# Where the inputs of a sign-weight MLP are made: before the MLP, or inside the attention ahead of it

## What is computed

```
x = x + cross_attention(layernorm(x), ctx, mask)      # x0
x = x + self_attention(layernorm(x))                  # s0: 16 heads of 32
x = x + sign_mlp(layernorm(x))                        # f0: the MLP of this change
x = x + cross_attention(layernorm(x), ctx)            # x1
x = x + causal_self_attention_rope(layernorm(x))      # s1
x = x + quantised_gated_mlp(layernorm(x))             # f1
```

```
h = concat([x, -x]);  h = relu(s0 * (h @ sign(k0))) * 2      # 1024 -> 2048
h = relu(s1 * (h @ sign(k1))) * 2                            # 2048 -> 2048
y = s2 * (h @ sign(k2))                                      # 2048 -> 512
layernorm(x) = (x - mean) / sqrt(var + 1e-5)
```

## Time and profile before

| what | us |
|---|---|
| median of three runs (lowest to highest) | 1258.74 (1256.92 to 1258.98) |
| span of the profiled execution, first to last instruction | 1256.4 |
| first self-attention, from its turn 0 to the last statistics | 201.5 to 317.3 |
| inputs of the sign MLP | 317.3 to 340.3 |
| its first layer on the first half | 340.3 to 379.6 |

### The profile page before, as it was taken

How to read it: one execution, slowest core, us unless ns; L and a number is a source line. 1 busy time by engine, 2 the same in 40 slices (tenths; PEclk the granted TensorE clock), 3 DMA queues, 4 the chain that set the end, 5 groups by cost and what they waited for, 6 DMA issues and landing times. The chain is left out here.

```text
span 1256.4 us, 18017 instructions
## 1 busy us (share of the span) xinstructions
PE 1117.3 (89%) x6536; PEld 684.3 (54%) x6536; DVE 597.6 (48%) x1030; ACT 364.9 (29%) x982; POOL 176.2 (14%) x173
## 2 busy tenths in 40 slices
PE   8999979998489999999998999968799999994986
PEld 4544437777234444444443655538477877863542
DVE  3133117888682111331111344337857566577766
ACT  1211124544221010121010122234333324245874
POOL 1011001110750000000000101104303131300004
PEclk9999988999589999999999999988899999997999
DMA  9964601000310000000001877833000000007001
GB/s 345 387 230 179 241 12 65 1 0 0 117 50 1 0 0 1 0 1 0 0 0 45 332 268 268 332 108 128 1 1 0 0 0 0 0 0 261 16 1 67
DMA packets 55122, 108.53 MB, mean 86 GB/s; under 512 B 4144, under 2 KB 4528, under 8 KB 55088
## 3 DMA queue, kind: packets, MB, share of 16 engines
q1 hardware_dynamic: 55088, 108.09, 24.0%
HBM read 105.98 MB, written 2.10 MB: 86 GB/s over the span
## 5 line engine op out<-in xcount | busy, mean ns | idle before, releaser
L1339 ACT ACTIVATE f_act<-bank,f_sgn 128x512 f32<-128x512 f32 x64 | 44.0, 687 | 273.6 <-PE bank L1296 258.0
L1296 PE MATMUL bank<-f_a_lo,f_w 128*128 128x512 f16 x512 | 115.7, 379 | 0.0
L1296 PE MATMUL bank<-f_a_hi,f_w 128*128 128x512 f16 x512 | 115.7, 379 | 0.0
L1392 DVE CAST f_b_hi<-f_act 128x512 f32 x32 | 13.7, 427 | 181.3 <-ACT f_act L1339 181.3
L962 ACT ACTIVATE s_e<-bank,s_nmax 128x64 f32<-128x64 f32 x256 | 76.0, 345 | 53.8 <-DVE s_nmax L1047 53.3
L1296 PEld LDWEIGHTS bank<-f_a_lo,f_w 128*128 x512 | 50.1, 98 | 60.4
L1296 PEld LDWEIGHTS bank<-f_a_hi,f_w 128*128 x512 | 50.1, 98 | 60.4
L526 POOL TENSOR_TENSOR x_mv<-x_mv,eps 128x2 f32<-128x2 f32 x8 | 1.5, 192 | 511.3 <-DVE x_mv L419 511.3
L1134 DVE TENSOR_TENSOR s_e<-s_pair,s_tables 128x512 f32<-128x512 f32 x64 | 41.3, 687 | 42.1 <-POOL s_kT L1197 24.8
L513 DVE TENSOR_TENSOR xres<-bank,xres 128x512 f32<-128x512 f32 (+1 forms) x16 | 11.1, 691 | 105.3 <-PE bank L332 91.5
L962 ACT ACTIVATION_READ_ACCUMULATOR s_e<-bank,s_nmax 128x1 f32 x256 | 60.9, 239 | 0.0
(11 more groups left out here) (259 smaller groups left out, 2232.1 us busy)
## 6 DMA issues: line engine op xcount, KB each, us to landing
x_cT<-in_ctx_cols_dram SPq DMA_DIRECT2D x32, 1024.0 KB, 7.6
x_cN<-in_ctx_rows_dram SPq DMA_DIRECT2D x32, 1024.0 KB, 10.0
f_upper_bits<-in_f_w_dram SPq DMA_DIRECT2D x20, 256.0 KB, 2.7
f_raw<-in_f_wd_dram SPq DMA_DIRECT2D x1, 2816.0 KB, 18.0
x_qw<-in_x_qw_dram SPq DMA_DIRECT2D x8, 256.0 KB, 4.2
x_kw<-in_x_kw_dram SPq DMA_DIRECT2D x8, 256.0 KB, 5.1
x_vw<-in_x_vw_dram SPq DMA_DIRECT2D x2, 1024.0 KB, 14.5
s_wk_ahead<-in_s_wk_dram SPq DMA_DIRECT2D x1, 2048.0 KB, 14.3
```

The lines of the kernel that those rows point to most:

```text
L1296: mm = pe.matmul(h_bank[s][:, :], weights(2 * i + s, k), part[:, k, cols], start=(n == 0 and k == 0), stop=(n == 1 and k == k_chunks - 1))
L1339: act.activation(act32[s][:, :], h_bank[s][:, :], ACT.Relu, scale=sgn[:, layer % 2:layer % 2 + 1]).then_inc(h_read, 1)
L1392: dve.tensor_copy(hi[:, 2 * i + s, :], act32[s][:, :]).then_inc(hhi_ok, 1)
```

## The change

Six of the eight tiles of the sign MLP's input are made inside s0. The statistics of the two tiles that a turn has finished are aggregated at the end of that turn on VectorE (new: a separating memset ahead of each statistics instruction, which the second self-attention gets too, one more memset, and two aggregations). At the start of the next turn GpSimd takes the root and normalises the two tiles into a new buffer `fn`; TensorE transposes them between the query and the value projections, into banks 2 and 3; ScalarE copies them to `fT_hi` after the queries; VectorE subtracts into `fT_lo` after `layernorm` and before the score maxima. TensorE waits for that before the scores of the second tile, which use the same banks. The last turn no longer normalises, transposes and splits tiles 0 and 1. Tiles 6 and 7 are normalised by GpSimd at the start of the sign MLP, and transposed, copied and split between layers 0 and 1 of the first half. GpSimd's order in s0 changes too: the root for the next turn's rows now stands ahead of the bias additions of this turn. s1 keeps its order but for the memsets.

```diff
@@ self_attention @@
+        F_BANK = [2, 3]
 @block.tensor
-            with pe.Fori(0, TILES // 2) as i:
+            def transpose_signs(n):
+                for s in range(2):
+                    pe.wait_ge(fn_ok, 2 * n + s + 1)
+                    for k in range(KC):
+                        mm = pe.transpose(bank[F_BANK[s]][:, k * P:(k + 1) * P], fn[s][:, k * P:(k + 1) * P], ident[:, :])
+                    mm.then_inc(fT_done, 1)
+            def turn(i, first, last):
...
                 project_transposed(i, PB, wq_hi, wq_lo, q_done, NB if rope is not None else base)
+                if sign_inputs is not None and not first:
+                    transpose_signs(i - 1)
...
                 if rope is None:
+                    if not first:
+                        pe.wait_ge(flo_ok, 2 * i)
                     scores(i, 1, range(GROUPS))
...
-                    transpose_x(i + 1)
+                    if not last:
+                        transpose_x(i + 1)
 @block.scalar
+                    if not first:
+                        for s in range(2):
+                            act.wait_ge(fT_done, 2 * i + s - 1)
+                            act.copy(fT_hi[:, :, bass.ts(2 * i + s - 2, P)], as_chunks(bank[F_BANK[s]][:, :])).then_inc(fhi_ok, 1)
 @block.vector
-                    layernorm(next_first, i + 1)
+                    if not last:
+                        layernorm(2 * i + 2, i + 1)
+                    if not first:
+                        for s in range(2):
+                            at = bass.ts(2 * i + s - 2, P)
+                            dve.wait_ge(fhi_ok, 2 * i + s - 1)
+                            dve.tensor_tensor(fT_lo[:, :, at], bank[F_BANK[s]][:, :].rearrange("p (k n) -> p k n", k=KC),
+                                              fT_hi[:, :, at], ALU.subtract).then_inc(flo_ok, 1)
...
-                    split_x(i + 1)
+                    if not last:
+                        split_x(i + 1)
...
                 for s in range(2):
                     dve.wait_ge(x_ok, 2 * i + s + 2)
-                    dve.bn_stats(core.stats[:, 2 * i + s, :], xres[:, 2 * i + s, :]).then_inc(next_stats, 1)
+                    dve.memset(core.spare[:, 4 + s:5 + s], 0.0)
+                    kept = core.stats[:, 2 * i + s, :] if sign_inputs is None or last else fstats[:, s, :]
+                    dve.bn_stats(kept, xres[:, 2 * i + s, :]).then_inc(next_stats, 1)
+                if sign_inputs is not None and not last:
+                    dve.wait_ge(next_stats, 2 * i + 2)
...
+                    dve.memset(core.spare[:, 6:7], 0.0)
+                    for s in range(2):
+                        dve.bn_aggr(fmv[:, s, 0:2], fstats[:, s, :]).then_inc(fvar_ok, 1)
 @block.gpsimd
+            def normalise_signs(n, first):
+                pool.wait_ge(fvar_ok, 2 * n + 2)
+                pool.tensor_tensor(fmv[:, :, 2], fmv[:, :, 1], core.eps[:, 0:1].to_broadcast([P, 2]), ALU.add).then_inc(frstd_ok, 1)
+                pool.wait_ge(frstd_ok, 2 * n + 1)
+                pool.tensor_tensor(fmv[:, :, 3], fmv[:, :, 2], core.minus_half[:, 0:1].to_broadcast([P, 2]), ALU.pow).then_inc(frstd_ok, 1)
+                pool.wait_ge(frstd_ok, 2 * n + 2)
+                for s in range(2):
...
+                    pool.tensor_scalar(fn[s][:, :], xres[:, 2 * n + s, :], fmv[:, s, 0:1], fmv[:, s, 3:4],
+                                       ALU.subtract, ALU.mult).then_inc(fn_ok, 1)
-            with pool.Fori(0, TILES // 2) as i:
+            def turn(i, first, last, second=False):
+                if sign_inputs is not None and not first:
+                    normalise_signs(i - 1, second)
+                if sign_inputs is not None and not last:
+                    rstd(i + 1)
                 for s in range(2):
                     pool.wait_ge(xn_ok, 2 * i + s + 1)
...
-                rstd(i + 1)
+                    rstd(i + 1)
@@ sign_mlp @@
 @block.tensor
...
             for half in range(HALVES):
+                if half == 1:
+                    pe.wait_ge(xhi_ok, 2)
+                    pe.wait_ge(xlo_ok, 2)
                 hidden(2 * half * HC, KC, lambda f, k: w0_sb[:, k, bass.ts(f, P)], xT_hi, xT_lo, slice(half * HT, (half + 1) * HT))
+                if half == 0:
+                    transpose_last()
 @block.gpsimd
-            pool.wait_ge(var_ok, TILES + 1)
-            pool.tensor_tensor(rstd[:, :], var[:, :], expo[:, :], ALU.pow).then_inc(rstd_ok, 1)
...
+            for s in range(2):
+                pool.tensor_scalar(xn[s][:, :], xres[:, TILES - 2 + s, :], mv[:, s, 0:1], rstd[:, s:s + 1],
+                                   ALU.subtract, ALU.mult).then_inc(xn_ok, 1)
```

More of the change, by code:

```diff
@@ L912, in _, with turn @@
                 act.wait_ge(set_ok, 3)
-            def turn(i, first):
+            def turn(i, first, last=False):
                 if rope is None:
@@ L1197, in _, with sign_mlp @@
                         pool.tensor_tensor(dst[:, 1, :], prods[1][:, 0, :], prods[0][:, 1, :], ALU.add).then_inc(rope_ok, 1)
-                rstd(i + 1)
-def sign_mlp(core, tag, w0_sb, bits, w1, w2, scales):
+                    rstd(i + 1)
+            if rope is None:
+                turn(0, True, False)
+                turn(1, False, False, second=True)
+                turn(2, False, False)
+                turn(3, False, True)
+            else:
+                with pool.Fori(0, TILES // 2) as i:
+                    turn(i, False, False)
+def sign_mlp(core, tag, w0_sb, bits, xT_hi, xT_lo, w1, w2, scales):
     nc = core.nc
@@ L1223, in sign_mlp @@
         raw = [bits[:, n, :] for n in range(RAW)]
-        xT_hi = sb("xT_hi", [P, KC, TOKENS], F16)
-        xT_lo = sb("xT_lo", [P, KC, TOKENS], F16)
         a_hi = sb("a_hi", [P, HC, HT], F16)
         a_lo = sb("a_lo", [P, HC, HT], F16)
+        with ExitStack() as early:
+            xn = [core.sbuf(early, f"{tag}_xn{s}", [P, D]) for s in range(2)]
         b_hi = sb("b_hi", [P, HC, HT], F16)
@@ L1327, in _ @@
             act.preload_act_table(ACT.Relu)
[L1328 to L1331, removed]
             act.wait_ge(sc, 6)
             for layer in range(2 * HALVES):
+                if layer == 1:
+                    for s in range(2):
+                        act.wait_ge(xT_done, s + 1)
+                        act.copy(xT_hi[:, :, (TILES - 2 + s) * P:(TILES - 1 + s) * P],
+                                 x_bank[s][:, :].rearrange("p (k n) -> p k n", k=KC)).then_inc(xhi_ok, 1)
                 with act.Fori(0, HC // 2) as i:
@@ L1346, in _ @@
             dve.memset(core.spare[:, 2:3], 0.0).then_inc(hlo_ok, 2)
[L1347 to L1352, removed]
+            for s in range(2):
+                dve.bn_aggr(mv[:, s, :], core.stats[:, TILES - 2 + s, :]).then_inc(var_ok, 1)
             dve.wait_ge(scales_in, 16)
@@ L1365, in _, with split_last @@
             dve.tensor_scalar(out_scale[:, :], s_abs[:, 3:4], s_in[:, 2:3], 4.0 * 2.0 / (SHIFT0 * SHIFT1), ALU.mult, ALU.mult).then_inc(sc, 1)
[L1366 to L1384, removed]
+            def split_last():
+                for s in range(2):
+                    dve.wait_ge(xhi_ok, s + 1)
+                    at = slice((TILES - 2 + s) * P, (TILES - 1 + s) * P)
+                    dve.tensor_tensor(xT_lo[:, :, at], x_bank[s][:, :].rearrange("p (k n) -> p k n", k=KC), xT_hi[:, :, at],
+                                      ALU.subtract).then_inc(xlo_ok, 1)
             for half in range(HALVES):
                 for layer in range(2):
+                    if half == 0 and layer == 1:
+                        split_last()
                     hi, lo = (a_hi, a_lo) if layer == 0 else (b_hi, b_lo)
```

77 lines of the change are left out of this document (58 added, 19 removed).

## The result

The changed kernel takes 1262.22 us (median of 8 runs, 1258.88 to 1264.77) against 1257.82 (8 runs, 1255.26 to 1258.98): ratio 1.0037, interval 1.0024 to 1.0049, some 4.6 us slower. The forecast was +3.0 us and 1261.7. The profiled execution's span went from 1256.4 to 1260.7. Each ratio in this document is to the kernel before as it ran beside the version in question (medians of 1257.82 here, 1256.86 for experiments 1 to 4, 1256.40 for 5 to 8), so two versions are compared "by the ratios" and not by their medians. One execution of experiment 2 took 1937.40 us at a mean granted clock of 0.553, and its ratio leaves it out.

A forecast was written before the change was run, and what follows sets the result against it. s0 was taken as bound by a closed chain of VectorE and ScalarE's exponentials, layer 0 by VectorE's contention with GpSimd. Sum: -6.3 + 5.6 + 2.6 + 0.8 + 0.3 + 0.5 - 0.5 = +3.0 us, 1261.7; range 1256.0 to 1266.5.

The forecast's parts named there:

- Layer 0 gains 7.2, with the transposes 6.3: Sign MLP, first half: layer 0 ends 7.2 us earlier; transposes of the last two tiles cost 0.9; sum -6.3 us.
- bounds 0.5 and 1.34, I take 0.5: MLP start: time of one GpSimd normalised row, taken as 0.5 us, so both tiles are hidden behind the arriving bytes.
- The scalars' rival: MLP start: seven tiny VectorE instructions run against GpSimd's expansions, two blocks fewer done: +3.5 us, 1265.2; chance 0.10.
- GpSimd's order, +5.6: s0, turns 0 to 2: bias additions hold up VectorE's normalised rows, 2.88 a pair instead of 1.00: 3 x 1.88 us.
- The rival that VectorE would get in first: s0: additions don't hold up the rows, so 5.6 falls away: -2.6 us, 1256.1, faster; chance 0.14.
- Splits, +2.6, and statistics, +0.8: s0, VectorE: split pair adds 1.28 in turns 1 and 2; aggregations and memsets add 0.4 in each of two turns.
- TensorE's wait hides in the chain: s0, turns 1 and 2: second tile's scores wait for splits, starting within 0.1 of the first maximum; no cost.
- The fall was named as a rival: TensorE's clock at half: +1.7 to +3.4 us in layer 0, as much again per turn in s0's longer waits; chance 0.15.
- One of the prediction's own signs of being wrong: s0: the forecast would be wrong if VectorE waits for TensorE ahead of the maxima of turns 1 and 2.
- GpSimd's rows for TensorE, "ready some 2.5 us after a turn's end": s0: GpSimd's normalised tiles are ready 2.5 us after a turn's end; TensorE wants them 6 us after it.
- Turn 3, +0.5, and the end, -0.5: s0: TensorE's transposes delay turn 3's maximum, +0.5 us; without the needless split the final output scaling is earlier, -0.5.
- s1's memsets, +0.3: Second self-attention: added statistics memsets cost at most 0.5 us, partly overlapped, taken as +0.3.

The follow-up runs named there:

- experiment 1: The changed kernel with GpSimd's bias additions ahead of the root again in s0: 1253.71 us, ratio 0.9978 to the kernel before.
- experiment 2: The kernel before with only GpSimd's order changed in s0, the root ahead of the bias additions: ratio 1.0048 to the kernel before.
- Experiment 3: The changed kernel with TensorE projecting the second tile's values ahead of its wait for the splits: ratio 1.0045 to the kernel before.
- experiment 4: The changed kernel with VectorE's two splits between the aggregation and the wait for the root: 1258.40 us, ratio 1.0013 to the kernel before.
- experiment 5: The changed kernel with GpSimd expanding four w1 pieces, the rest after VectorE finishes layer 0 of the first half: 1242.67 us, ratio 0.9889 to the kernel before.
- experiment 8: The changed kernel with bias additions first, splits before the root wait, and twelve w1 expansions held behind layer 0: 1231.15 us, ratio 0.9804 to the kernel before.

## Why the prediction was right, and where it was off

The direction and the main reasons held; the size of s0 was short by 3.4 us. That the time came out within 2 us of the forecast is in part luck: s0 and the stretch to layer 1 together grew by 6.0 in the profiles where 2.7 were forecast, and what lies behind them happened to be 2.4 shorter, 1.6 of it in x1, which the change doesn't touch.

*Layer 0 gains 7.2, with the transposes 6.3.* Measured 6.4, and experiment 5 shows that VectorE's contention with GpSimd is what keeps 21 us of earlier start from being more. But two errors cancel in it. The step that priced GpSimd's rows, "bounds 0.5 and 1.34, I take 0.5", was wrong: they take 2.1 each. The expansions therefore began 5.6 us behind the memset, not 4.3, and ended at 48.7, not 47.7; in return VectorE had started both instructions of block 0 before the first of them (0.43 and 0.69), and had eleven blocks done at their end where the prediction had ten. The scalars' rival did not come of it in this profile: GpSimd was still at its rows (333.25 to 337.4) when the seven scalars ran from 334.61 on, and they took 0.14 to 0.21 each, as before. But little was to spare: in experiments 4 and 8, where they started 0.3 later behind the memset, three of them took 0.37 to 0.55, block 0's cast met the first expansion, and a block was lost.

*GpSimd's order, +5.6.* Right: 2.9 a pair in all three turns, and experiments 1 and 2 show it from both sides (-9.2 in s0 with the clock's share, +6.9 for four turns without slow scores, 1.7 each). The row in x0 had the exact price. The rival that VectorE would get in first did not occur in any turn of any run with the new order.

*Splits, +2.6, and statistics, +0.8.* The turn 1 step of +3.2 holds rows, splits and aggregation together, 3.56 forecast. With the order restored (experiment 1) s0 is 3.3 us above the kernel before, where these terms with the +0.5 and the -0.5 of turn 3 make 3.4. One by one, by differences of starts in the changed kernel's timeline: the pair of splits moves the maxima by 1.20 in turns 1 and 2 (1.28 forecast), and from the statistics to the next keys it takes 1.55 and 1.90 where it took 1.20 and 1.19, so +0.35 and +0.7 (0.4 each forecast).

*TensorE's wait hides in the chain.* This is the step that failed. I had the splits' wait leave the second tile's scores "within 0.1 of the first maximum" and costed it at nothing; their start was as forecast (247.27 against a maximum at 247.14), but the wait itself was 2.2 us long in a place where TensorE had none, its clock went to the lower level, and the scores took 3.5 us. The fall was named as a rival and given a place in the range, but not in the sum. From the first maximum to the next split takes 13.4 us in turn 1 and 13.3 in turn 2 against 11.6 and 11.9 before: +1.7 and +1.4, the 3.1 of the missing 3.4. Experiment 3 shows that filling the wait keeps the scores at 1.95 and brings 1.7 us back in turn 1, and experiments 1 and 4, where the wait is 0.3 to 0.8 or gone, have no slow scores. One of the prediction's own signs of being wrong, VectorE waiting for TensorE at the maxima of turns 1 and 2, was thereby half met: the first maximum did not wait, the third and fourth did. When the clock falls is not settled by these runs. It fell at both waits for splits in the changed kernel and in experiment 5, whose s0 is the same. Behind waits of 1.7 us for exponentials it fell in turn 0 of experiment 2 and turn 2 of experiments 3 and 4, but not in turn 0 of the changed kernel or turn 1 of experiments 3 and 4.

*GpSimd's rows for TensorE, "ready some 2.5 us after a turn's end".* Mis-sized for the same reason as in the MLP: they are ready 5.3 us after it (the end of the aggregations). It cost nothing, since TensorE came to them 5.6 to 6.2 us after it, but only 0.3 us was to spare in turn 2.

*Turn 3, +0.5, and the end, -0.5.* From TensorE's first projection to the maxima of turn 3 it took 16.25 us against 15.73, +0.5 as forecast; the rest of the +1.9 in the table is turn 2's slow scores. The end gave 0.2.

*s1's memsets, +0.3,* can't be told apart: s1 takes 296.5 to 298.4 us in the three profiles without them and 296.2 to 298.0 in the seven with them.

## What to carry to other kernels

Before filling a gap in front of a stage, look at what paces the stage: here it was a helper engine's work list that started at a fixed time, one held VectorE instruction per GpSimd instruction, and 21 us of earlier start were worth 6.4. With most of that list moved behind the stage on both sides, the same step was worth 15.2. If an engine's order is rewritten, look for the same order elsewhere in the trace; the additions behind the root in x0 told the price of the new order to 0.1 us. And a wait put into TensorE's stream can cost even when the chain doesn't wait for it: ask how long it is, and what the next instructions take at half the clock.

## What was not expected of the hardware

- A GpSimd instruction with one 128x512 f32 input and two per-partition scalars takes 2.1 us, also while VectorE is nearly idle; the two-input addition of the same shape takes 1.34, and the expansion of 128x2048 bytes with two constants 2.0.
- TensorE's granted clock fell to its lower level behind waits of 2.2 and 3.0 us in an otherwise busy turn, and the following sixteen products took 3.5 in place of 1.95. Shorter waits, of 1.7, went with a fall in three turns and without one in others.
- In layer 0, with 1.73 us of work every 4.3, the clock changes between its levels, and which one holds when the stage speeds up moved layer 1 by 0, 1.7 or 1.8 us between four profiles whose MLP code is the same.
- Three VectorE instructions of 128x2 and 128x3 f32 took 0.15 to 0.17 us beside GpSimd's rows in the changed kernel and 0.37 to 0.55 in experiments 4 and 8, where they started 0.3 later.
